# A gated cross-attention and top-2 expert block: routed tiles in one pass, and in two

## What is computed

```
x = x + tanh(g_xattn) * attention(layernorm(x), ctx, ctx)       # per sequence; Wq, Wk, Wv, Wo
n = layernorm(x)
scores = softmax(n @ gate_w + gate_b);  top 2 of 8 experts
for i in range(8):                                              # out is overwritten, not summed
    y = relu((n * w_i) @ w1[i] + b1[i]) @ w2[i] + b2[i]
    out = where(w_i > 0, y, out)
x = x + tanh(g_ffn) * out
```

## Time and profile before

| | us |
|---|---|
| median of 3 runs | 188.35 |
| profiled execution, its own time | 188.17 |
| its span, first to last instruction | 186.1 |
| busy: PE / DVE / ACT / POOL | 136.0 / 120.7 / 90.3 / 91.0 |

### The profile page before, as it was taken

The page is one execution under the profiler, slowest core; times in us unless marked ns, Lnnn a source line. Parts: engine busy times, 40 slices in busy tenths (PEclk is TensorE's granted clock), DMA queues, the critical chain, the costliest instruction groups (busy, mean ns, idle before and its releaser), DMA issues.

```text
span 186.1 us, 5245 instructions
## 1 busy us (share of the span) xinstructions
PE 136.0 (73%) x1685; PEld 109.1 (59%) x1685; DVE 120.7 (65%) x380; ACT 90.3 (49%) x208; POOL 91.0 (49%) x133
## 2 busy tenths in 40 slices
PE   7489786999988989989683501000999999999930
PEld 2074444678666767667452300000999999999930
DVE  5585848546689989999774778510266667576520
ACT  1277770015587887787781100002466676576300
POOL 8384899743264540604107376760034455455460
PEclk9858999555799999999999655555599999999995
DMA  4965976754024034544410002521112222221100
GB/s 121 264 203 158 241 198 170 207 150 108 21 61 121 7 130 137 195 138 152 161 41 30 30 15 64 164 62 41 50 43 58 65 59 54 72 65 55 30 0 0
DMA packets 17992, 18.34 MB, mean 99 GB/s; under 512 B 2944, under 2 KB 15747, under 8 KB 17952
## 3 DMA queue, kind: packets, MB, share of 16 engines
q1 hardware_dynamic: 15104, 14.50, 27.6%
q0 software_dynamic: 1280, 2.25, 3.9%
q10 hardware_dynamic: 1584, 1.29, 2.6%
HBM read 8.80 MB, written 3.26 MB: 65 GB/s over the span
## 4 chain that ended last, share of the span: by engine, by line
PE 52%; DVE 10%; POOL 9%; ACT 9%; issue 7%; DMA 6%; another core or an unknown queue 2%; ACTq 1%; SPq 1%; DVEq 0%; POOLq 0%
PE pair L1157 12%; POOL rows_dram L517 6%; PE bank L1167 6%; PE pair L1167 6%; PE bank L1071 5%; ACT probs L654 4%; DMA value_pack<-in_value 4%; PE pair L1043 4%; PE pair L1056 3%; PE bank L1117 3%; PE pair L987 3%; DVE smax L798 2%; PE pair L1028 2%; DVE routed L783 2%
## 5 line engine op out<-in xcount | busy, mean ns | idle before, releaser
L798 DVE TENSOR_REDUCE smax<-pair 128x8 f32<-128x1024 f32 x32 | 39.5, 1309 | 7.3 <-PE pair L1056 7.2
L565 POOL DMA_INDIRECT out<-ctxT,tokens x23 | 23.4, 1019 | 33.1 <-DVE ctxT L963 18.6
L654 ACT ACTIVATE probs<-pair 128x1024 f32<-128x1024 f32 x32 | 32.5, 1015 | 11.5 <-PE pair L1043 11.5
L1157 PE MATMUL pair<-ctxT,q_stack 128*128 128x128 f32 x184 | 25.9, 287 | 0.0
L1157 PEld LDWEIGHTS pair<-ctxT,q_stack 128*128 128x128 f32 x184 | 24.0, 204 | 0.0
L517 POOL DMA_INDIRECT rows_dram<-routed,rowpos x16 | 15.9, 994 | 14.2 <-DVE routed L897 9.1
L956 DVE TENSOR_SCALAR q_stack<-pair,q_stack 128x128 f32<-128x128 f32 x46 | 13.9, 344 | 12.6 <-PE pair L1157 12.6
L700 ACT ACTIVATE q_stack<-pair,q_stack 128x128 f32<-128x128 f32 x46 | 14.4, 365 | 15.4 <-PE pair L1157 15.4
L690 ACT ACTIVATE q_stack<-q_stack 128x128 f32<-128x128 f32 x23 | 11.3, 492 | 20.3 <-DMA q_stack<-rows_dram 19.9
L1149 PE MATMUL pair<-first_pack,q_stack 128*128 128x128 f32 x23 | 6.8, 294 | 17.2 <-ACT q_stack L690 16.4
L1071 PE MATMUL bank<-probs,vall 128*18 128x128 f32 x512 | 18.0, 283 | 0.6 <-ACT probs L654 0.6
(11 more groups left out here) (167 smaller groups left out, 277.0 us busy)
## 6 DMA issues: line engine op xcount, KB each, us to landing
wexp<-in_wexp SPq DMA_DIRECT2D x8, 514.0 KB, 3.4
k_stack<-k_part SPq DMA_DIRECT2D x24, 128.0 KB, 2.7
q_stack<-q_part SPq DMA_DIRECT2D x24, 128.0 KB, 2.9
q_stack<-rows_dram SPq DMA_DIRECT2D x23, 68.5 KB
x<-in_x SPq DMA_DIRECT2D x4, 256.0 KB, 7.4
ctxT<-in_ctxT SPq DMA_DIRECT2D x3, 256.0 KB, 7.4
out<-ctxT,tokens POOLq DMA_INDIRECT x23
late_pack<-in_late ACTq DMA_DIRECT2D x1, 329.5 KB, 5.2
```

Of the source, the lines that this page charges most:

```text
L565: pool.indirect_dma_start(io["out"], bass.IndirectOffsetOnAxis(ap=tokens[t % R][:, :].bitcast(u32), axis=0), result[t % R], None, bounds_c ...
L654: nc.scalar.activation(probs[s % 2][:, t].rearrange("p h g q -> p (h g q)"), shifted_pair[:, :], ACT.Exp, scale=HD ** -0.5).then_inc(s_exp, 1)
L798: V.reduce_max(smax[q % 2][:, :, CHUNK * t:CHUNK * (t + 1)], score_pair[t][:, :].rearrange("p (h g k) -> p h g k", h=2, g=CHUNK), axis=AX.X)\
L1157: ins = M(out, w1cur[k.u][:, c * P:(c + 1) * P], rowsT[k.u], start=True, stop=True)
```

## The change

- The expert tiles run in two passes. Pass 0 has the tokens of sequences 0 to 3 in 4 + 7 = 11 tiles, pass 1 those of sequences 4 to 15 in 12 + 7 = 19. Each pass has its own `rows_dram`, table, pad rows and semaphores. The groups in which routing is computed stay 0 to 7 and 8 to 15.
- Table and pad rows of pass 0 are made inside the attention pipeline: counts and table in step 18 on DVE (`tile_counts`, `tile_table`), after `row_places(0)` in step 17; `row_weights(0)` moves from step 17 to 16. In step 19 DVE copies the w1 of the first three tiles.
- Group 1's routing lies among the first tiles: `gate_exp(1)` on ACT after tile step 1, `rank(1)` on PE at tile step 3, `tile_counts(1)` and `tile_table(1)` on DVE after tile steps 6 and 8. On DVE everything up to `row_places(1)` still comes ahead of its tile steps.
- All pads are issued by SP: pass 0's after `row_places(0)`, pass 1's before the load of tile 6. ACT issues none.
- For the first three tiles ACT does all of the relu. The copy of w1 moves from the start of a tile's step 0 to the end of the step before.
- POOL scatters sequences 0 to 3 as before, then the other twelve, then stores results.
- All engines' tile steps are written out; there is no loop left.

```diff
-GROUPS = ((0, 8), (8, 16))
+SPLIT = 4
+GROUPS = ((0, 8), (8, SEQS))
+PASSES = ((0, SPLIT), (SPLIT, SEQS))
...
+PASS_TILES = tuple(end - first + EXPERTS - 1 for first, end in PASSES)
+TILES = sum(PASS_TILES)
...
-        RANK_STEP = 17
+        RANK_STEP, TABLE_STEP, W1_STEP = 17, 18, 19
+        W1_AHEAD, PADS_TILE, TABLE_TILES = 3, R, (6, 8)
+        GEXP_TILE, RANK_TILE, ACT_TILES = 1, 3, 3
...
+        def pads(eng, g):
+
+            for e in range(EXPERTS):
+                first = eng.value_load(pad_rows[g][0:1, e:e + 1], min_val=0, max_val=EXPERTS * CAP)
+                eng.dma_start(rows_dram[g][ds(first, P), :], spare).then_inc(s_pad[g], 16)
...
             sp.wait_ge(s_padrow, 1)
             pads(sp, 0)
-            sp.wait_ge(s_pad, 16 * EXPERTS)
-            sp.wait_ge(s_spare, 16)
-            sp.wait_ge(s_scat, 16 * SEQS)
-
-            sp.wait_ge(s_tab, 1)
-            def load_tile(item):
+            sp.wait_ge(s_spare, 32)
+            sp.wait_ge(s_s2, HALVES * SEQS)
+
+            def load_tile(n, item):
                 if t := item(0):
-                    first = sp.value_load(tab[0:1, ds(t.no + TILES, 1)], min_val=0, max_val=EXPERTS * CAP)
+                    if t.no == PADS_TILE:
+                        sp.wait_ge(s_padrow, 2)
+                        pads(sp, 1)
+                    if t.place == 0:
+                        sp.wait_ge(s_pad[t.turn], 16 * EXPERTS)
+                        sp.wait_ge(s_tab, t.turn + 1)
+                        first, end = PASSES[t.turn]
+                        sp.wait_ge(s_scat[t.turn], 16 * (end - first))
+                    at = PASS_TILES[t.turn] + t.place
+                    first = sp.value_load(tab[t.turn][0:1, at:at + 1], min_val=0, max_val=EXPERTS * CAP)
                     wait(sp, s_res, t.no - R + 1)
-                    sp.dma_start(rows[t.u], rows_dram[ds(first, P), :]).then_inc(s_tile[t.u], 16)
-            experts(sp, load_tile)
+                    sp.dma_start(rows[t.u], rows_dram[t.turn][ds(first, P), :]).then_inc(s_tile[t.u], 16)
+            experts(load_tile)
...
-            scatter(0, 2)
+            scatter(0, SPLIT)
             invert_std(2)
-            scatter(2, 4)
+            scatter(SPLIT, SPLIT + 2)
             invert_std(LAST)
-            scatter(4, 8)
+            scatter(SPLIT + 2, GROUPS[1][0])
...
-            gate_exp(1)
-            act.wait_ge(s_padrow, 1)
-            pads(act, 1)
...
-                    for c in range(2):
+                    for c in range(HC if k.no < ACT_TILES else 2):
...
+                if n == GEXP_TILE:
+                    gate_exp(1)
...
                 if n == RANK_STEP:
                     row_places(0)
-                    row_weights(0)
                 if n in STATS_STEP:
                     second_stats(STATS_STEP[n])
+                if n == TABLE_STEP:
+                    tile_counts(0)
+                    tile_table(0)
+                elif n == W1_STEP:
+                    dve.wait_ge(s_wexp, 16 * EXPERTS)
+                    dve.wait_ge(s_s2, HALVES * SEQS)
+                    for k in range(W1_AHEAD):
+                        place_w1(k)
                 if n == SEQS:
                     second_choice(0)
+                    row_weights(0)
...
+            def place_w1(no):
+
+                t = Item(no)
+                dve.wait_ge(s_tab, t.turn + 1)
+                e = dve.value_load(tab[t.turn][0:1, t.place:t.place + 1], min_val=0, max_val=EXPERTS - 1)
+                wait(dve, s_down, no - R + 1)
+                wait(dve, s_rv, no - R + 1 - ACT_TILES)
+                V.tensor_copy(w1cur[t.u], wexp[:, ds(e, 1), HC * D:WROW].rearrange("p a w -> p (a w)")).then_inc(s_w1, 1)
...
+            def expert_step(n, item):
+                if (k := item(LAG_UP)) and k.no >= ACT_TILES:
...
+                if n >= LAG_UP and n + 1 < TILES:
+                    place_w1(n + 1)
+                if n == TABLE_TILES[0]:
+                    tile_counts(1)
+                elif n == TABLE_TILES[1]:
+                    tile_table(1)
...
-            rank(1)
-
-            pe.wait_ge(s_tab, 1)
             pe.wait_ge(s_wexp, 16 * EXPERTS)
             pe.wait_ge(s_b2, 1)
-            def expert_step(item):
+            def expert_step(n, item):
+                if n == RANK_TILE:
+                    pe.wait_ge(s_x1, SEQS)
+                    rank(1)
```

More of the change, by code:

```diff
@@ L41 @@
 HC = HID // P
-CAP = TOKENS + P
-TILES = TOKENS // P + EXPERTS - 1
+CAP = max(end - first for first, end in PASSES) * QLEN + P
+PASS_TILES = tuple(end - first + EXPERTS - 1 for first, end in PASSES)
+TILES = sum(PASS_TILES)
+MOST_TILES = max(PASS_TILES)
 RW = DX + 1
@@ L64, in build @@
     ds = bass.ds
[L67 removed]
+    rows_dram = [nc.dram_tensor(f"rows_dram{g}", [EXPERTS * CAP + P, RW], fp32, kind="Internal").ap() for g in range(2)]
     with ExitStack() as ctx:
@@ L290, in build, with __init__ @@
         class Item:
[L293 to L313, removed]
+            def __init__(self, no):
+                self.no, self.u, self.lap, self.no2 = no, no % R, no // R, no % 2
+                self.turn = no >= PASS_TILES[0]
+                self.place = no - self.turn * PASS_TILES[0]
         LAG_MT, LAG_S2, LAG_PV, LAG_HT, LAG_OUT = 1, 3, 4, 5, 6
         LAG_TURN, LAG_UP, LAG_DOWN = 1, 2, 3
-        RANK_BANKS = (None, 0)
-        EXPERTS_FIRST = 11
-        assert (TILES - EXPERTS_FIRST) % R == 0 and EXPERTS_FIRST >= LAG_DOWN + R - 1
         def attention(one_step):
@@ L365, in group_ranks @@
             first, end = GROUPS[g]
-            width = end - first + (end == SEQS)
-            out = dve_bank[:, 392:] if g == 0 else bank[RANK_BANKS[g]]
-            return out[:, 0:width * EXPERTS].rearrange("p (t e) -> p t e", e=EXPERTS)
+            width = end - first + 1
+            return dve_bank[:, 392:392 + width * EXPERTS].rearrange("p (t e) -> p t e", e=EXPERTS)
         block = ctx.enter_context(nc.Block())
@@ L547, in _ @@
                 elif n == 9:
-                    pool.dma_start(rows_dram[EXPERTS * CAP:EXPERTS * CAP + P, :], spare).then_inc(s_spare, 16)
+                    for g in range(2):
+                        pool.dma_start(rows_dram[g][EXPERTS * CAP:EXPERTS * CAP + P, :], spare).then_inc(s_spare, 16)
                 elif n == 11:
@@ L908, in row_places @@
                 V.tensor_copy(rowpos[:, at], top[:, at]).then_inc(s_routed, 1)
-                if end == SEQS:
-                    V.tensor_copy(pad_rows[:, :], ranks[0:1, end - first, :]).then_inc(s_padrow, 1)
-                    order.after(V.tensor_tensor(count[:, :], ranks[:, end - first, :], region, ALU.subtract))
+                order.after(V.tensor_tensor(count[:, :], ranks[:, end - first, :], region, ALU.subtract))
+                V.tensor_copy(pad_rows[g][:, :], ranks[0:1, end - first, :]).then_inc(s_padrow, 1)
@@ new lines, in tile_counts @@
+            def tile_counts(g):
+                order.after(V.tensor_scalar(ntiles_i[:, :], count[:, :], float(P - 1), None, ALU.add))
+                order.after(V.tensor_scalar(ntiles_i[:, :], ntiles_i[:, :], 7, None, ALU.arith_shift_right))
+                order.after(V.tensor_copy(ntiles[:, :], ntiles_i[:, :]))
+                E88 = [P, EXPERTS, EXPERTS]
+                order.after(V.tensor_tensor(tab8[:, :, :], upto, ntiles[:, :].unsqueeze(1).to_broadcast(E88), ALU.mult))
+                V.tensor_scalar(adjust[:, :], ntiles[:, :], -float(P), float(CAP), ALU.mult, ALU.add)
+                order.after(V.reduce_sum(ends[:, :], tab8[:, :, :], axis=AX.X))
@@ L921, in _ @@
             row_places(1)
-            order.after(V.tensor_scalar(ntiles_i[:, :], count[:, :], float(P - 1), None, ALU.add))
-            order.after(V.tensor_scalar(ntiles_i[:, :], ntiles_i[:, :], 7, None, ALU.arith_shift_right))
-            order.after(V.tensor_copy(ntiles[:, :], ntiles_i[:, :]))
-            E88 = [P, EXPERTS, EXPERTS]
-            order.after(V.tensor_tensor(tab8[:, :, :], upto, ntiles[:, :].unsqueeze(1).to_broadcast(E88), ALU.mult))
-            order.after(V.reduce_sum(ends[:, :], tab8[:, :, :], axis=AX.X))
```

127 lines of the change are left out of this document (61 added, 66 removed).

## The result

The kernel after took 200.38 us (median of 4 runs, 199.41 to 201.28), the kernel before beside it 188.27 (186.84 to 189.06): ratio 1.065, interval 1.056 to 1.074. The forecast was 192.8, its range ended at 197. The profiled execution took 199.61, span 197.7. Ratios and intervals leave out executions more than 1.5% above the fastest of the same kernel, the medians keep them, so the two need not agree to the last half per cent.

The account below looks back on a forecast made before the run. PE bounds the tiles at 2.005 us each. Product 1 16.4 us earlier, seven tiles 14.0, tile 6 5.2, table 1.4, 0.2 rounding: 4.4 us later, 192.8 us; likeliest 191 to 194.5, 8 in 10 187.2 to 197.

Parts of the forecast that it names:

- Seven tiles, 14.0 us: Tile train on PE: 30 tiles instead of 23, 2.005 us each, adding 14.0 us with no cover.
- VectorE in the attention, 3.4 us late: Attention steps 16 to 19: pass 0's table and w1 copies make DVE's x1 and group 1's choice 3.4 us late.
- Tile 0 released by the pads, 110.8: First tiles: pass 0's pads, landing at 108.1, release tile 0, which ACT scales at 110.8.
- Product 1 at 116.5: PE's tile step 3: up product 1 follows group 1's choice and ranks, at 116.5 against 132.94, 16.4 us earlier.
- Tile 6, 5.2 us (5.1 to 9): Ahead of up product 5: tile 6's load queues on SP behind eight pads, stalling PE 5.2 us, ends 5.1 and 9.
- The clock: Rival: PE's clock restarts slowly after tile 6's wait, 1.6 us more, 194.4; chance 0.20.
- The table, 1.4: Tile steps 6 to 9: pass 1's table on DVE delays tile 7's relu, costing PE 1.4 us.
- Pass 1's gate, no stall: Tile 11: pass 1's table comes last, at 138.3; tile scaled at 141.0 for PE's step at 142, no stall.
- The tail: After the last up product: everything as before, no cost.
- The other side: Rival, tile steps 6 to 9: side engines' slack covers pass 1's routing, saving 6.8 us, 186.0; chance 0.14.

Follow-up runs that it names:

- first pair: Kernel before and kernel after as first measured and traced side by side, a disturbed session; 188.27 and 200.38 us, ratio 1.065.
- quiet pair: Unchanged repeats without standstill: kernel before again (185.78 us, span 183.7) and kernel after, fourth run (196.38 us, span 193.9, ratio 1.061).
- e4: Kernel after, with POOL's last eight scatters waiting until pass 1's pads have landed; 194.74 us, 1.049, and 195.78 us, 1.057, of before, both quiet.
- e3: Kernel after with 64 one-column matmuls ahead of PE's first product, shifting PE's code; 194.86 us, 1.049 of before; disturbed 200.16 us, 1.064.
- e10: Kernel after; loads 6 to 9 each followed by one SP pad, four pads and first w1 copies on ScalarE, exponential behind tile 0; quiet 187.68 us, disturbed 197.52.
- e11: Kernel after with 64 already satisfied waits on SP ahead of its attention loop, shifting SP's code; 204.41 us, 1.070 of before, disturbed.
- e12: e10 with the 15 operations of pass 1's table three at a time behind tile steps 3 to 7; 196.10 us, 1.038 of before, disturbed.
- e2: Kernel after with pass 1's odd four pads on ScalarE behind its third tile step; 192.07 us, 1.034, and 192.71 us, 1.038, of before.
- e9: Kernel after with 50 matmuls into an idle bank ahead of PE's wait for tile 6; 194.40 us, 1.044 of before.
- e7: Kernel after with two pads behind each of loads 6 to 9 and w1 copies of tiles 0 to 2 on ScalarE; 188.68 us, 1.016 of before.

## Why the prediction was wrong, step by step

- *Seven tiles, 14.0 us:* right to 0.03 (39.99 - 25.96).
- *VectorE in the attention, 3.4 us late:* near in the first pair (chosenb from 112.07 to 115.95, 3.9), but by a cover that was not there to keep: the 2.66 us wait of the earlier trace rows that "hides most" of the table was for the most part a standstill. In the quiet pair the cover is 0.54 and the term is 5.2 to 5.7. It is in product 1's -14.8 for -16.4.
- *Tile 0 released by the pads, 110.8:* 110.54, and 109.78 quiet. Product 1 at 116.5: 116.83, or 117.0 as the chain counts.
- *Tile 6, 5.2 us (5.1 to 9):* the step that failed, by size. The mechanism and its place are as told, the wait is 7.6 quiet, 7.9 with its step. Its pieces, in the chain's starts: load to scaled row 3.29 us (126.77 to 130.06) where I took 1.84 from a load with the queues empty, +1.45, and e4 shows that the scatters in flight make 1.3 of it; from the pad rows to product 4 PE needs 4.8, not 5.5, since its clock had recovered by then, +0.7; from the scaled row to product 5 1.2 for 0.8, +0.4; the pads +0.1 (load issued 10.2 after the pad rows, for 10.05). The upper end, 9, came from pads "1.6 apart"; the earlier trace rows give (4.87 - 0.36) / 3 = 1.5, and so 8.2. The pads came 1.19 apart on average.
- *The clock:* I costed a restart at nothing and kept it as a rival at 0.20 and 1.6 us. It is 2.3 in this pair and 1.4 in e3, which does the same work in the same order (products 5 to 7 in 6.28 and 5.38 us for 4.0). The row that spoke for it, 4.6 us of low work before the fall against a forecast wait of 5.2, was on the table and should have decided.
- *The table, 1.4:* 1.4, 1.3 in the first pair. *Pass 1's gate, no stall:* right in after; it shows only once the stall is gone (e10).
- *The tail:* costed at nothing, 0.5 quiet and 1.2 first, not followed further.
- *The standstill:* not in the forecast, and one was in its profile. What it adds to after can't be told (12.1 and 12.4 us over before, for 10.7 and 12.5 quiet; the intervals overlap); it adds 2.8 to e3 and 7.2 to e10.

The terms that failed are thus one wait (+2.7), its restart (+2.3) and VectorE's delay (+1.6), with 0.5 of tail, less 1.1 for products 1 to 4 at a recovered clock and 0.2 at the table: 5.8 us, from the 4.4 forecast to the 10.2 of the quiet pair. The seven tiles and the table stand. The other side (186.0, under before) was not reached: with SP's pads spread and the w1 copies off VectorE, e10 comes from 10.7 us over before to 2.0, and there the waits that are left are small; the 14.0 us of tiles and most of VectorE's delay stay.

## What to carry to other kernels

Count an issue with a register address as an engine's time (1.1 us here), and compare the sum over a steady period with that period: two extra issues per 2.0 us tile are a bound wherever they stand. A stall that the change itself makes is priced with its restart. And look at an idle time that is to serve as cover in more than one trace, and follow it back: here a wait on "remote" two steps up the chain was the sign that it would be gone in another session.

## What the runs showed of the hardware

- In disturbed sessions ScalarE waits 3.3 (before) and 4.8 to 5.0 us (two passes) at the attention's last product instead of 1.2. In two-pass kernels SP, PE, ScalarE and VectorE stand still a second time between up products 3 and 4, where a wait of 4.8 to 7.1 us of ScalarE ends between 129.4 and 133.7, and in after SP's small steps take 0.7 us each there instead of 0.33. The waits on "remote" are in every trace of a session with a before of 188.3 to 188.9 (seven; in the kernel before only the first) and in none of the others (thirteen). The cause is open: another place of PE's code (e3 twice) or SP's (e11) does not take it away, and it is there without a row of pads (e10, e12); scatters held back from the pads were not tested where it occurs.
- A tile load took 1.9 us from its issue to its reader with quiet queues, 2.0 with pads but no scatters in flight (e4), 3.0 to 3.3 behind eight pads and beside scatters, and 4.6 to 4.9 in e2, where two engines issue pads.
- In e9 the granted clock fell at about 132, when the short idle time ahead of tile 6 (1.8 us) was over and PE was at full work again. In e2 it fell behind waits of 2.8 and 3.3 us, in e7 behind one of 2.1.
